# V products of an attention pair in three groups of four key blocks, in slots 3, 7 and 12

## The reference

```python
q = (xn @ q_w + q_b).reshape(b, s, H, HD).transpose(0, 2, 1, 3)   # H = 16 heads, HD = 64
k = (xn @ k_w + k_b).reshape(b, s, H, HD).transpose(0, 2, 1, 3)
v = (xn @ v_w + v_b).reshape(b, s, H, HD).transpose(0, 2, 1, 3)
q = _rope(q, theta)
k = _rope(k, theta)
scores = jnp.einsum('bhqd,bhkd->bhqk', q, k) * scale
scores = jnp.where(causal, scores, -jnp.inf)
attn = jax.nn.softmax(scores, axis=-1)
ctx = jnp.einsum('bhqk,bhkd->bhqd', attn, v)
ctx = ctx.transpose(0, 2, 1, 3).reshape(b, s, H * HD)
attn_out = ctx @ o_w + o_b + xn
```

## Time and profile before

| | |
|---|---|
| median of 3 runs | 2342.74 us (2339.05 to 2348.59) |
| profiled execution | 2338.65 us, span 2336.8 us |
| TensorE matmuls | 1966.5 us busy, 84% of the span |
| VectorE | 1682.9 us, 72% |
| ScalarE | 1461.8 us, 63% |
| GpSimd | 892.5 us, 38% |
| V products (L1397) | 1536 passes, 289.3 us busy |

### The profile page before, as it was taken

One profiled execution on the slowest core, in us unless ns is written; L12 is line 12 of the kernel. 1 busy time (PEld: TensorE's weight loads), 2 busy tenths in 40 slices (PEclk: granted clock), 3 DMA queues, 4 the chain that ended last, 5 costly groups with the idle time before them and its releaser, 6 DMA issues.

```text
span 2336.8 us, 42183 instructions
## 1 busy us (share of the span) xinstructions
PE 1966.5 (84%) x9942; PEld 1301.4 (56%) x9942; DVE 1682.9 (72%) x3031; ACT 1461.8 (63%) x2909; POOL 892.5 (38%) x907
## 2 busy tenths in 40 slices
PE   3759999879775999979967699996996769998798
PEld 1236676557324676746732567664662356676466
DVE  4867777579487777757948777775894877777588
ACT  3528777557453777846744477774674457777476
POOL 1554435033165353413315634431232564353222
PEclk9879999979797999998979799998997989999899
DMA  2011101011001111101100111100100011110011
GB/s 77 0 29 34 41 21 37 1 32 40 24 1 41 26 37 34 25 10 32 31 24 1 41 35 27 40 18 12 34 27 25 0 41 42 25 36 18 19 32 32
DMA packets 65411, 64.49 MB, mean 28 GB/s; under 512 B 12184, under 2 KB 48384, under 8 KB 65280
## 3 DMA queue, kind: packets, MB, share of 16 engines
q1 hardware_dynamic: 65280, 63.01, 10.3%
HBM read 27.31 MB, written 2.10 MB: 13 GB/s over the span
## 4 chain that ended last, share of the span: by engine, by line
PE 55%; DVE 19%; issue 12%; ACT 9%; POOL 3%; ACTq 1%; DVEq 1%; DMA 1%; SPq 0%; POOLq 0%
PE ps L1397 10%; PE ps L1236 6%; PE ps L1238 6%; PE ps L1237 6%; PE ps L1386 6%; DVE state L966 6%; PE ps L1376 4%; PE ps L1377 3%; ACT probsT L741 3%; ACT probs L729 2%; PE ps L1505 2%; PE ps L1264 2%; PE ps L1360 2%; ACT ps L706 2%; DVE bx L959 1%
## 5 line engine op out<-in xcount | busy, mean ns | idle before, releaser
L729 ACT ACTIVATE probs<-ps,least 128x640 f32<-128x640 f32 (+7 forms) x512 | 379.8, 742 | 102.9 <-DVE least L1052 87.2
L741 ACT ACTIVATE probsT<-ps 128x512 f32<-128x512 f32 (+3 forms) x768 | 347.6, 490 | 91.0 <-PE ps L1386 81.1
L1386 PE MATMUL ps<-ident,probs 128*128 128x128 f32 x2304 | 350.6, 277 | 11.5 <-ACT probsT L741 5.9
L1376 PE MATMUL ps<-k_high,q_split 128*128 128x512 f32 (+3 forms) x768 | 302.2, 393 | 55.1 <-DVE q_split L1042 33.3
L1386 PEld LDWEIGHTS ps<-ident,probs 128*128 128x128 f32 x2304 | 271.1, 141 | 52.9 <-ACT probsT L741 28.4
L1397 PE MATMUL ps<-probsT,vals 128*64 128x512 f32 (+3 forms) x1536 | 289.3, 500 | 3.7 <-ACT probsT L741 3.7
L1059 DVE TENSOR_REDUCE least<-ps 128x1 f32<-128x640 f32 (+3 forms) x256 | 262.3, 1024 | 8.8
L1377 PE MATMUL ps<-k_low,q_split 128*128 128x512 f32 (+3 forms) x768 | 260.5, 351 | 0.0
L1376 PEld LDWEIGHTS ps<-k_high,q_split 128*128 128x128 f32 x768 | 146.8, 191 | 177.1 <-ACT probs L729 91.8
L791 ACT ACTIVATE hid<-ps,cols 128x512 f32<-128x512 f32 x256 | 176.3, 689 | 102.9 <-PE ps L1238 74.5
L478 POOL TENSOR_SCALAR inverse_wide<-inverse 128x512 f32<-128x512 f32 x64 | 39.6, 618 | 520.8 <-DVE inverse L1063 519.3
(11 more groups left out here) (210 smaller groups left out, 4013.4 us busy)
## 6 DMA issues: line engine op xcount, KB each, us to landing
roped<-turned SPq DMA_DIRECT2D x512, 64.0 KB, 2.0
w<-in_w SPq DMA_DIRECT2D x128, 128.0 KB, 2.0
w_pair<-in_w_pairs SPq DMA_DIRECT2D x36, 128.0 KB, 2.6
xin<-in_x SPq DMA_DIRECT2D x5, 512.0 KB, 3.9
out<-acc SPq DMA_DIRECT2D x4, 512.0 KB, 4.1
pos<-in_c_pos SPq DMA_DIRECT2D x1, 512.0 KB, 4.8
v_w<-in_v_w SPq DMA_DIRECT2D x1, 512.0 KB
o_w<-in_o_w SPq DMA_DIRECT2D x1, 512.0 KB
```

Of the source, the lines that this page charges most:

```text
L729: act.activation(probs[:, t % 2, 0:width(t)], banks(2 * (t % 2))[:, 0:width(t)], ACT.Exp, bias=least[:, t:t + 1], scale=-1.0, accum_out=ro ...
L741: act.activation(dst, ps[:, T_BANK + g % 2, 0:k1 - k0], ACT.Copy).then_inc(t_taken, 1)
L1376: pe.matmul(o, q, k_high[par][h][:, k0:k1], start=True, stop=False)
L1386: made = pe.transpose(ps[:, T_BANK + g % 2, at - k0:at - k0 + P], probs[:, t % 2, at:at + P], ident[:, :])
```

## The change

```diff
--- before.py
+++ after.py
@@ -98,7 +98,7 @@
 PROLOGUE_BANK = (7, 4, 5, 6)
 V_AT = (9, 10)
 SPREAD_AT, OUTPUT_AT = (12, 8), (14, 11)
-PV_NEW_AT, PV_OLD_AT = (11, 12), (1, 3, 5, 7)
+PV_NEW_AT, PV_OLD_AT = (12,), (3, 7)
 
 NORM_AT = (0, 1, 2, 4, 6)
 SUM_SLOT = 3
```

## The result

The change made the kernel slower: 2371.86 us (median, 2364.34 to 2374.60), against 2342.01 us for the kernel before on the same chip. The ratio is 1.0127 by the medians; the estimate from all runs of both is 1.012, with a 95% interval of 1.0092 to 1.0147. Forecast were 2357.7 us, +15; measured is +30 (+29 from the 2342.74 that the forecast started from), twice as much. The range of 2338 to 2372 holds the result by 0.14 us.

The account below looks back on a forecast made before the run. It took TensorE, busy 225.48 of 233.00 us, as the main bound, with V products covering VectorE's chain. Middle pairs 24 x 0.80 = +19.2, first -1.4, last -2.8: +15 on median 2342.74, so 2357.7 us; range 2338 to 2372.

Parts of the forecast that it names:

- the walk: Middle pair followed slot by slot: stalls 2.53 us, less 1.05 of group overhead, less 0.65 of old wait: +0.83, taken as +0.80.
- The worked bounds: Over all pairs: +0.25 to +1.3 us per middle pair, +2 to +27 us in all, 2345 to 2370.
- The chain bare before g1: Slot 2's projection waits for VectorE's sine, minimum, cosine behind slot 0's; a 1.68 us stall replaces the slot 1 group.
- S(7), g3, S(9): Unit 7's scores (slot 5) stall 0.30 us, slot 6's projection stalls 0.55, unit 9's scores (slot 7) come 1.83 later.
- Slots 8 to 10: Second value projection waits for VectorE, behind by only 1.1 us; 0.65 of wait is used up, leaving TensorE 1.18 later.
- Slots 11 to 15: Unit 13's scores shift by -0.57 us, unit 14's come 0.81 later; everything up to the next pair stands some 0.8 late.
- Group overhead of 0.35: Each group of V products costs TensorE 0.35 us beyond its passes; three groups per middle pair are removed, 1.05.
- First pairs: First pair of each batch changes only in slots 11 and 12: 4 x -0.35 = -1.4 us.
- last pairs: VectorE's input norm holds slot 3, so slots 1 and 3 give nothing; two other merges give 4 x -0.70 = -2.8 us.
- TensorE as the whole bound: Rival for the whole kernel: the saved 31 us of TensorE time come off, giving 2311.6 us; chance 0.12.
- the lateness is absorbed in slots 13 to 15: Rival: these slots hang on ScalarE's wait in slot 12, so 0.80 becomes 0; only -4.2 stays, 2338.5 us; chance 0.13.
- The clock falling: Rival: thinned slots 0 to 2 put some 3.4 us per middle pair at half clock, costing 41 us, to 2399; chance 0.08.

Follow-up runs that it names:

- the padded sine: One unused 256-column VectorE product put ahead of the sine of slot 0's projection: changed kernel 2386.47 us, ratio 1.0208; kernel before 2349.96 us, 1.0046.
- the sum moved: Changed kernel with GpSimd's last sum of rotated halves put behind its copy that widens the inverses: 2359.49 us, ratio 1.007 to the kernel before.
- Half 0 merged alone: Kernel before with only the new half's V products merged, slots 11 and 12 into 12; old half stays in slots 1, 3, 5, 7: 2335.47 us, 0.9992.
- The version with one block per slot: Kernel before with the old half's eight blocks one in each of slots 0 to 7; slots 11 and 12 unchanged: 2387.73 us, ratio 1.0203.
- the version between the two: Kernel before with old blocks 0, 1 in slot 1, 2, 3 in slot 3, 4 to 7 in slot 7, new half in slot 12: 2327.61 us, 0.9957.

## Why the forecast was right in its sign and half its size

The forecast had the way right: the groups covered a chain on VectorE. What failed is one term of its sum, the lateness at the second value projection, 1.18 in the walk: it is 2.13 in the pair followed, and 16 of the 24 middle pairs are like it. That the result still lies in the range is luck in part. The worked bounds ended at +27 us, and only the few us put on for the spread of runs take in the +30. And the long product's 15 us were partly made up for by pairs 1 and 2, which the forecast had too short before the change.

**The chain bare before g1: right.** +3.07 forecast and measured. The idle in front of it is 1.05, the row's shape is that of the first pair in the earlier trace rows, and the padded sine shows that VectorE sets it.

**S(7), g3, S(9): right** to 0.11 (10.52, 11.88, 16.19). The stall before S(7) is the 0.30 forecast.

**Slots 8 to 10: the mis-sized term.** The forecast read VectorE as behind by only 1.1 in this place and took TensorE's lateness there for 1.18, after 0.65 of old wait. It measured 2.13 in the fourth pair and 1.24 in the third. The values of that projection start 19.72 behind g0 before the change and 21.84 after it, and 20.83 with the sum moved: without the long product VectorE is behind by 1.11, as forecast. The walk moved VectorE's instructions at fixed durations and set them beside TensorE alone. It didn't ask where GpSimd's stand when VectorE's slot 8 moves. The warning was in the trace of the kernel before: the product of slot 8 had 0.51 us to spare ahead of the sum (290.82 against 291.33), and that of slot 7 was held already (1.00). After the change the one comes 1.17 later, the other 0.52. The bounds of the forecast took in a wait more or less, but no instruction that gets longer. 0.95 x 16 pairs is 15.2 us, and the moved sum gave back 15.6 in these pairs. (In the walk 2 x 0.43 + 2 x 0.32 is 1.50, not 1.49; nothing hangs on it.)

**Slots 11 to 15: right.** From the second value projection to the next pair the walk has 15.56, measured are 15.59. S(13) to S(14) is 4.38, forecast 4.29. ScalarE's two waits, foretold as 2.51 to 0.3 and a new one of 1.4, are 0.64 and 1.53.

**Group overhead of 0.35: right.** Half 0 merged alone gives 0.33 per pair.

The Trainium skill's "TensorEngine Tiling (Array Packing)", section "Key Properties", with its drain at a change of mode, is borne out by that, but it prices no cover. The version with one block per slot shows the other side: four groups more cost 1.64 per pair, where their overhead is 1.40 and 0.65 of it was to be absorbed; the rest goes with what they delay (g1 by 0.62).

**The other pairs.** Pairs 1 and 2 grew by 0.35 and not 0.80: they were 36.85 long on average before, not 36.39, as their product of slot 7 was held for longer, and came to the 37.2 of the walk. For the eight pairs that is 3.6 us less than forecast. First pairs gained nothing, where 1.4 were forecast, and why is open; last pairs gave 4.2, where 2.8 were, within their spread. The sum of the parts in the profiled executions is +2.8 + 28.3 + 0.1 - 4.2 - 1.3 (everything else) = +25.7, the growth of the span. The medians are 4 further apart, which is within what these parts vary by.

**The rivals.** TensorE as the whole bound is out, since the chain on VectorE sets g1. That the lateness is absorbed in slots 13 to 15 is out: what VectorE is late by at the second value projection reaches the next pair to 0.03. The clock falling is out for this change: it stood at 1.00 over the middle pairs. No run shows the 3.4 us per pair at half clock by which the forecast priced it. It did fall in the padded kernels, elsewhere.

## What to carry to other kernels

Before work is taken out of a slot, ask what it covers: the two blocks in slot 1 hid VectorE's chain between two projections that share one PSUM bank, and three overheads of 0.35 did not pay for that. When a change shifts one engine against another, put the instructions of all engines on one scale at their new times, VectorE's with two SBUF inputs and GpSimd's above all: 0.65 us of shift between the two changed a product from 0.73 to 1.68 us. And merge where nothing hangs on the cover: two blocks kept in slots 1 and 3, four in slot 7 and one group in slot 12 are faster than either kernel, by 0.43% against the one before, though a part of that may be the order of product and sum in slot 7.

## What the runs showed that was not expected

**A product behind a GpSimd instruction.** It ends some 0.55 us after that instruction does: 1.68 behind a sum of 1.27 that began 0.14 earlier, 1.15 behind a copy of 0.61 that began 0.01 earlier. GpSimd's durations in these rows stay at 1.27 and 0.61. It holds throughout the traces of both kernels: 28 of the 128 products before the change and 40 after it start while a sum runs, and all of them end 0.54 to 0.65 after it. When VectorE is first, it is GpSimd's that stretches: the sum of slot 8 took 1.36 before the change, that of slot 7 takes 1.70 in the version between the two.

**The clock in first pairs.** Both kernels with the padded sine lost 2.8 to 2.9 us in each of their four first pairs. Stretches of the second batch's first pair, the kernel before and the padded one (columns as in the earlier trace rows):

```profile
744.00:748.00 4.00, 3.30 (x18) 2.32 (x16) 3.13 (x7) 2.69 (x8) 2.90 (x3) 1.00 0.30 70
748.00:752.00 4.00, 2.06 (x10) 1.47 (x10) 3.46 (x7) 3.40 (x9) 3.02 (x4) 1.00 0.36 86
752.00:756.00 4.00, 3.12 (x20) 2.37 (x19) 3.73 (x7) 3.78 (x8) 3.43 (x3) 1.00 0.32 78
```

```profile
752.00:756.00 4.00, 3.08 (x17) 2.26 (x16) 3.13 (x7) 2.34 (x7) 1.11 (x1) 1.00 0.32 74
756.00:760.00 4.00, 1.11 (x6) 0.69 (x5) 2.42 (x5) 2.38 (x6) 3.13 (x4) 1.00 0.25 61
760.00:764.00 4.00, 3.57 (x13) 3.05 (x14) 2.46 (x6) 2.36 (x7) 3.54 (x3) 0.57 0.20 49
```

In the middle stretch TensorE was busy 2.06 us in the one and 1.11 in the other. Behind it the granted clock stayed at 1.00 in the one and was 0.57 in the other (0.5 is the 1.2 GHz level). The idle came from a DMA. GpSimd's sum, which stands 6.72 behind g0 in the kernel before, came 8.4 to 8.9 behind it in all eight first pairs of the padded kernels:

```profile
756.22 1.26 POOL L565 TENSOR_TENSOR roped<-turned,roped 128x512 f32<-128x512 f32 x1 [3.11 <-DMA roped<-turned]
...
758.76 0.50 PE L1379 MATMUL ps<-k_high,q_split 128*128 128x512 f32 x1 [2.71 <-ACT probs L730]
```

The scores after it waited 2.71 us, where they waited 1.33 before. The four DMAs of the swap are issued only 0.32 later than in the kernel before, and the first three land 0.32 later. The fourth is the one that is late: it lands 8.1 to 8.7 behind g0 in the eight first pairs, where it landed at 6.5 in the four of the kernel before. The trace has one 16 KB packet of the instruction queue in each of these places. It starts 6.0 to 6.2 behind g0 in the padded kernels, while the fourth DMA's packets run (from 6.05 in the pair shown), and takes 0.9 to 1.5 us; 45 of that DMA's 48 packets are through at 6.49, and it lands only after the instruction packet has ended (at 7.55). In the same pair of the kernel before, the fourth DMA's last packet starts at 6.18 and the instruction packet at 6.21, and it is the next DMA that lands late, at 8.7, for which this sum doesn't wait.

So the padding itself costs 0.3 of the 2.8 us per first pair. The rest goes with a DMA that it shifted beside an instruction packet, the idle behind that, and the fallen clock. This is read from the order in time alone; no run moved the packet.
